# A grouped convolution ahead of a Strassen-like matrix product: the outer blocks of the convolution as one wider product in another bank, added by VectorE

## What is computed

```python
conv = lax.conv_general_dilated(x, weight, (1,), padding=[(4, 4)],      # x (32,128,2048), weight (128,32,9)
                                feature_group_count=4)                  # 4 groups of 32 channels, 9 taps
y = conv + einsum('nd,od->no', cond, c_weight)[:, :, None] + conv_bias[None, :, None]
base = matmul(y, kernel) + ffn_bias                                     # kernel (2048, 2048)
delta = B_eff @ (A_eff @ y) + lora_B_shared @ (lora_A_shared @ y)       # low rank parts, rank 32, per batch of 4 samples
out = x + base + delta
```

## Time and profile before

| | us |
|---|---|
| median of 3 runs | 1742.2 (1741.74 to 1744.91) |
| the profiled execution | 1747.0, span 1745.2 |
| TensorE busy | 1722.7 (99%) in 8666 matmuls |
| VectorE busy | 987.1 (57%) in 1260 instructions |
| ScalarE busy | 669.9 (38%) |
| mean granted clock of TensorE | 0.996 |

### The profile page before, as it was taken

One profiled execution on the slowest core, in us unless ns is written; L12 is line 12 of the kernel. 1 busy time (PEld: TensorE's weight loads), 2 busy tenths in 40 slices (PEclk: granted clock), 3 DMA queues, 4 the chain that ended last, 5 costly groups with the idle time before them and its releaser, 6 DMA issues.

```text
span 1745.2 us, 21990 instructions
## 1 busy us (share of the span) xinstructions
PE 1722.7 (99%) x8666; PEld 1460.6 (84%) x8666; DVE 987.1 (57%) x1260; ACT 669.9 (38%) x846; POOL 36.1 (2%) x70
## 2 busy tenths in 40 slices
PE   9999999999999999999999999999999999999998
PEld 6778888887888889999999888888888888888887
DVE  7647766664444578777665544355455554464443
ACT  6656666654222376555561221132233211121110
POOL 0001200000000000000000000000000000000000
PEclk9999999999999999999999999999999999999999
DMA  7859876656665656766665676568667798887764
GB/s 229 249 152 334 291 260 234 230 201 196 225 226 198 226 204 258 271 254 241 247 244 200 213 247 222 188 200 269 217 224 228 274 333 303 305 322 259 241 240 158
DMA packets 180143, 419.48 MB, mean 240 GB/s; under 512 B 50692, under 2 KB 90212, under 8 KB 175400
## 3 DMA queue, kind: packets, MB, share of 16 engines
q1 hardware_dynamic: 169960, 381.22, 64.1%
q0 software_dynamic: 9216, 33.56, 5.2%
q10 hardware_dynamic: 864, 3.29, 0.5%
HBM read 271.97 MB, written 146.03 MB: 240 GB/s over the span
## 4 chain that ended last, share of the span: by engine, by line
PE 89%; DMA 5%; DVE 3%; ACT 1%; issue 1%; SPq 0%; POOL 0%; ACTq 0%; DVEq 0%
PE acc L1430 65%; PE cps L1306 15%; PE acc L1337 3%; PE cps L1353 3%; DMA g<-in_L_ffn_kernel 2%; DMA T<-g 1%; DMA g<-in_L_ffn_lora_A 1%; ACT x_q L688 1%; PE acc L1385 1%; PE cps L1370 1%; DMA mixed_A<-g 1%; DVE x_q L946 0%; DMA st<-in_L_ffn_kernel 0%; DMA b_raw<-shared_B 0%; PE cps L1363 0%
## 5 line engine op out<-in xcount | busy, mean ns | idle before, releaser
L1430 PE MATMUL acc<-w_hi,y_t 128*128 128x512 f32 x3584 | 996.0, 392 | 1.8 <-DVE w_lo L938 1.8
L1430 PEld LDWEIGHTS acc<-w_hi,y_t 128*128 128x128 f32 x3584 | 666.5, 188 | 138.4 <-issue 2.7
L1430 PE MATMUL acc<-w_lo,y_t 128*128 128x512 f32 x1792 | 553.8, 390 | 0.0
L1430 PEld LDWEIGHTS acc<-w_lo,y_t 128*128 128x128 f32 x1792 | 337.2, 188 | 71.5
L688 ACT COPY x_q<-x_raw 32x512 f32<-32x512 f32 x248 | 268.4, 1082 | 16.2 <-DVE x_lo L952 13.4
L1306 PE MATMUL cps<-cw_hi,x_hi 128*128 128x384 f32 (+2 forms) x768 | 229.7, 299 | 3.3 <-DVE ax L1085 2.6
L1063 DVE TENSOR_TENSOR g<-acc,g 128x1024 f32<-128x1024 f32 x96 | 117.2, 1222 | 203.8 <-PE acc L1337 116.7
L1306 PE MATMUL cps<-cw_lo,x_hi 128*128 128x384 f32 (+2 forms) x768 | 229.8, 299 | 0.0
L1306 PE MATMUL cps<-cw_hi,x_lo 128*128 128x384 f32 (+2 forms) x768 | 229.2, 298 | 0.0
L727 ACT CAST y_t<-g 128x1024 fp32r<-128x1024 f32 x95 | 100.1, 1054 | 334.8 <-PE acc L1430 305.4
L1023 DVE TENSOR_TENSOR y_t<-g,y_t 128x1024 fp32r<-128x1024 f32 x95 | 116.0, 1221 | 109.8 <-ACT y_t L727 109.6
(11 more groups left out here) (117 smaller groups left out, 940.7 us busy)
## 6 DMA issues: line engine op xcount, KB each, us to landing
g<-A SPq DMA_DIRECT2D x80, 512.0 KB, 4.7
g<-U SPq DMA_DIRECT2D x80, 512.0 KB, 6.2
A<-g SPq DMA_DIRECT2D x64, 512.0 KB, 4.8
g<-in_x SPq DMA_DIRECT2D x64, 512.0 KB, 6.3
out<-g SPq DMA_DIRECT2D x64, 512.0 KB, 3.5
x_raw<-in_x SPq DMA_DIRECT2D x31, 1024.0 KB, 5.2
U<-g SPq DMA_DIRECT2D x48, 512.0 KB, 3.9
g<-in_L_ffn_kernel POOLq DMA_DIRECT2D x32, 512.0 KB, 8.6
```

What stands on the lines that cost most here:

```text
L1430: ins = T.matmul(acc[:, b, m, :], y_buf[b][:, c, part, :], wt[:, k % SLOTS, m * 512:(m + 1) * 512], start=(c == 0 and part == 0 and wt is ...
```

## The change

In 28 of the 32 convolutions (all but v = 0, 1, 16 and 17) the products of x_hi with both parts of the weights are taken out of the two outer blocks. `cw_hi` and `cw_lo` become the two halves of one buffer, so that a moving operand of 2x128 columns takes both parts; `apart(v, i)` does one such matmul for each outer block, into `acc[:, v % 2, i % 2]`, the bank pair that is not in use by product(v - 1). The remaining 14 matmuls of a group go into `cps` as before (of the outer blocks, x_lo with cw_hi).

The order on TensorE: groups 0 and 1, `apart` 0, group 2, `apart` 1, group 3, `apart` 2, `apart` 3. `apart` i now raises `conv_done`. There are two banks for four groups, so `apart` 2 and 3 wait until `y_evac` says that groups 0 and 1 were taken.

On VectorE each `y_group` gets two more operations: after L962 it adds the columns of the high part of the weights and then those of the low part, 128x256 each, to the two ends of the group's `y_conv`. Each waits for the one ahead of it, by `y_added`; the last raises `y_evac`.

```diff
+OUTER = (5, 0)
...
-        cw_hi = sb("cw_hi", [P, GR, 3, P], F32R)
-        cw_lo = sb("cw_lo", [P, GR, 3, P], F32R)
+        cw = sb("cw", [P, 2, GR, 3, P], F32R)
...
+        cw_hi, cw_lo = cw[:, 0], cw[:, 1]
+        cw_both = cw[:].rearrange("p a g d m -> p a g (d m)")
...
+        def outer_apart(v):
+            return v not in (0, 1, NP, NP + 1)
+        def added_index(v):
+            return v - 2 if v < NP else v - 4
...
                                 ctx_bias[:, v % 2, gr * GC:(gr + 1) * GC].unsqueeze(1).to_broadcast([P, WIN, GC]),
-                                ALU.add).then_inc(y_evac, 1)
+                                ALU.add).then_inc(y_added if outer_apart(v) else y_evac, 1)
+                if outer_apart(v):
+                    ends = y_conv.rearrange("p (a t) o -> p a t o", t=4)[:, 0:4:3, :, gr * GC:(gr + 1) * GC]
+                    apart = acc[:, v % 2, i % 2, :].rearrange("p (a h t o) -> p a h t o", a=2, h=2, o=GC)
+                    for part in range(2):
+                        dve.wait_ge(y_added, (2 * GR) * added_index(v) + 2 * i + part + 1)
+                        V.tensor_tensor(ends, apart[:, :, part], ends, ALU.add).then_inc((y_added, y_evac)[part], 1)
...
+            def apart(v, i):
+                gr = GROUPS[i]
+                if i >= 2:
+                    pe.wait_ge(y_evac, 4 * v + i - 1)
+                elif v < NP:
+                    pe.wait_ge(evac_act, v - 1)
+                else:
+                    pe.wait_ge(evac_dve, v - 1)
+                for blk, row, col, k0, k1, t0 in TAPS_OF:
+                    if blk in OUTER:
+                        n = 0 if t0 == 0 else 256
+                        ins = T.matmul(acc[:, v % 2, i % 2, n:n + 256], x_hi[:, gr, row, col:col + P],
+                                       cw_both[:, :, gr, k0 * GC:k1 * GC], start=True, stop=True)
+                ins.then_inc(conv_done, 1)
...
+                    if outer_apart(v) and i >= 2:
+                        apart(v, i - 2)
+                    n, last = 0, 13 if outer_apart(v) else 17
+                    for blk, row, col, k0, k1, t0 in TAPS_OF:
                         for xs, ws in ((x_hi, 0), (x_hi, 1), (x_lo, 0)):
+                            if outer_apart(v) and blk in OUTER and xs is x_hi:
+                                continue
                             ins = T.matmul(cps[:, gr, t0 * GC:(t0 + k1 - k0) * GC], xs[:, gr, row, col:col + P],
-                                           cw_strip[ws][:, gr, k0 * GC:k1 * GC], start=(n == 0), stop=(n == 17))
+                                           cw_strip[ws][:, gr, k0 * GC:k1 * GC], start=(n == 0), stop=(n == last))
                             n += 1
+                    if outer_apart(v):
+                        continue
...
+                if outer_apart(v):
+                    apart(v, 2)
+                    apart(v, 3)
```

More of the change, by code:

```diff
@@ L131, in build @@
         axd_words = axd_hl[:].bitcast(F32)
-        cw_strip = [w[:].rearrange("p g d m -> p g (d m)") for w in (cw_hi, cw_lo)]
+        cw_hi, cw_lo = cw[:, 0], cw[:, 1]
+        cw_strip = [w.rearrange("p g d m -> p g (d m)") for w in (cw_hi, cw_lo)]
+        cw_both = cw[:].rearrange("p a g d m -> p a g (d m)")
         wraw = b_raw[:, 0:GC * TAPS].rearrange("p (i k) -> p k i", k=TAPS)
@@ L239, in build @@
         y_evac = sem("y_evac")
+        y_added = sem("y_added")
         yc_out = [sem("yc_out0"), sem("yc_out1")]
@@ L1302, in conv @@
                         pe.wait_ge(ax_ready, NP + v - 1)
-                    n = 0
-                    for _, row, col, k0, k1, t0 in TAPS_OF:
+                    if outer_apart(v) and i >= 2:
+                        apart(v, i - 2)
+                    n, last = 0, 13 if outer_apart(v) else 17
+                    for blk, row, col, k0, k1, t0 in TAPS_OF:
                         for xs, ws in ((x_hi, 0), (x_hi, 1), (x_lo, 0)):
+                            if outer_apart(v) and blk in OUTER and xs is x_hi:
+                                continue
                             ins = T.matmul(cps[:, gr, t0 * GC:(t0 + k1 - k0) * GC], xs[:, gr, row, col:col + P],
-                                           cw_strip[ws][:, gr, k0 * GC:k1 * GC], start=(n == 0), stop=(n == 17))
+                                           cw_strip[ws][:, gr, k0 * GC:k1 * GC], start=(n == 0), stop=(n == last))
                             n += 1
+                    if outer_apart(v):
+                        continue
                     ins.then_inc(conv_done, 1)
```

## The result

The changed kernel takes 1791.1 us (median of 4, 1787.3 to 1791.8) against 1742.0 (median of 4, 1741.0 to 1744.9): ratio 1.0279, 95% interval 1.0265 to 1.0293, 2.8% slower. 1785 was forecast, with a range of 1766 to 1805. The profiled execution took 1791.4 with a span of 1789.6, against 1747.0 and 1745.2 before. The profiled execution of the kernel before lies 5 us above its kernel's median, so the spans differ by 44.4 and the medians by 49.1.

What follows compares the result with a forecast made beforehand. TensorE, busy 99% of the span, was taken to bound the kernel. Waits net of the saving, 29.7 us, plus 13.6 of clock loss gave 43, added to 1742.2: 1785 us, range 1766 to 1805.

Steps and rivals of the forecast that it cites:

- The saving: TensorE's outer blocks: one 256-column matmul replaces two of 128, saving 0.90 us per convolution, 25 us over 28.
- VectorE's price: Two dependent adds per group: 1.53 us from group to group, convolution ends 3.52 us after the emptying starts.
- Y stays: Y, from the start of L1135 (T) to VectorE's emptying, stays; only the forms' DMA waits, 16.5 us, get hidden.
- The sum of the waits: TensorE waiting for freed banks in the third and fourth wider products, saving included: +29.7 us over all convolutions.
- the old 4.7: v = 4 to 8 of the kernel before: 4.7 us of other waits, behind late emptyings or late forms, that go.
- The clock: TensorE's granted clock falls after idle gaps ahead of the third wider product: 13.6 us lost.
- the six long gaps: TensorE idling 2.5 to 5.4 us in v = 4 to 7, 10 and 13: 4x2.6+2x1.6 = 13.6 us of clock loss.
- the five short ones: TensorE idling 1.3 to 1.8 us in v = 8, 9, 11, 12, 14: taken as nothing, left open up to 8 us.
- The periods: Sign in the profile after, L1135 to L1135: 27 to 29 us in v = 4 to 7, 25 to 27 in v = 9 to 14.
- waits, but the clock stays up: Rival: TensorE waits for the banks but its granted clock does not fall; +30, 1772 us; chance 0.25.
- The clock falls in the short gaps too: Rival: short gaps also lower TensorE's clock, or the adds take longer than 0.424 us; 1803 us; chance 0.15.
- The wait never binds: Rival: emptying starts before T+5.3, T being L1135's start, and the saving is paid in full; -25, 1717 us; chance 0.03.

Runs made afterwards that it cites:

- e8: Changed kernel with VectorE's eight sample copies set between the groups' emptyings and the forms moved ahead of copy_mixed_B: 1721.7 us, ratio to the kernel before 0.9855.
- e10: Changed kernel with one VectorE add for each group in place of two, TensorE's work the same: 1763.4 us, ratio to the kernel before 1.0109.
- e3: Changed kernel with 151 useless matmuls filling TensorE's idle time ahead of the third wider product in v = 4 to 14: 1772.4 us, ratio to before 1.0158.
- e11: Changed kernel with useless matmuls filling the short gaps only, in v = 9, 11, 12 and 14: 1786.8 us, ratio to the kernel before 1.0246.
- e4: Changed kernel with VectorE's eight copies of the next sample set between the groups' emptyings: 1735.0 us, ratio to the kernel before 0.9940.
- e7: Kernel before, all 18 matmuls and no wider product, plus only VectorE's two adds and their waits in the 28 convolutions: 1748.9 us, ratio 1.0023.
- e9: Changed kernel with only the forms moved ahead of copy_mixed_B on VectorE, nothing interleaved: 1745.1 us, ratio to the kernel before 1.0005.

## Why the prediction was right, step by step

- **The saving.** 0.90 us a convolution was forecast, 25 in all; without waits it is 0.81 in phase 2 (9.69 to 8.88 in e8) and 0.80 in phase 0, 22.5 in all. The two wider products of a group take 0.29 us from their first start to the next other matmul in e8 (702.09 to 702.38), not 2x0.118. That alone would take 0.21 off the 0.90; what gives back 0.12 is not shown. The 81 ns of the Trainium skill ("TensorE: Matmul & The Clock Gate", Back-to-back issue gap) would have given 10 us, an estimate from the page. This case's traces do not agree with it: the row of before, 0.115 us for 128 columns, was the better guide.
- **VectorE's price.** 1.53 from group to group and 3.52 from the start of the emptying to product were both met to 0.01 us where the clock was up. They came out of two errors of opposite sign: release to matmul took 0.06 (362.68 to 362.74), forecast 0.15, and the two matmuls after a wait took 0.34, forecast 0.24. e10 shows the adds' part: two fewer in the chain, 0.9 us less.
- **Y stays.** In the changed kernel L1154 still waits 5.43 us in every period from v = 4 on, and L974 follows it by 7.9 to 9.5 us in v = 8 to 14, the same as before in v = 9 to 14 (v = 8 started at T+13.8 before). The DMA wait of the forms, 16.5 us, is 0 in v = 5 to 8, as forecast.
- **The sum of the waits.** v = 4 to 8: forecast 16.0, the convolutions grew by 21.2 and the old 4.7 went, 16.5. v = 9 to 14: forecast 13.8, measured 14.8 (in v = 9, 10, 11 and 13 the last two wider products took 0.54 to 0.60 us up to product's start, not 0.34, since the clock fell within them). v = 18 to 30: forecast 2.5, measured 1.8. The idle times themselves were 0.3 to 0.5 us shorter than forecast (1.0 to 1.5 in the short cases, not 1.3 to 1.8), since the main matmuls ended at T+8.5 and not at T+8.3, and TensorE started 0.1 us sooner after the release.
- **The clock: the term that was mis-sized.** 13.6 was forecast for the six long gaps (with 2.6 for each of four, where its row gave 2.7) and nothing for the five short ones; measured from what lies between the convolutions (13.54 before), the long ones lost 11.1 (1.1 to 2.6 each) and four of the short ones 5.8, 16.8 together. The prediction left the short gaps open and then put them at nothing; that is the step that failed. The 0.24 us of work between two gaps did not protect in ten of eleven periods. e3 shows the whole term by taking it away, 19.0 us with what was lost within the convolutions, e11 the part of the short gaps. The price itself was less certain than one row suggests: the gap of 2.65 us at convolution 16, from which the 1.6 was read, stands in every run and cost nothing in the changed kernel, e4, e7 and e9, 1.5 to 1.6 in the kernel before and six others, and 2.8 to 3.0 in e8 and e10. First matmul of convolution 16 and of product in the changed kernel, then in e8:

```profile
666.61 0.59 PE L1345 MATMUL cps<-cw,x_hi 128*128 128x384 f32 x2 [2.65 <-DVE ax L1104]
...
676.39 0.68 PE L1474 MATMUL acc<-w_hi,y_t 128*128 128x512 f32 x2
...
611.43 0.98 PE L1362 MATMUL cps<-cw,x_hi 128*128 128x384 f32 x2 [2.64 <-DVE ax L1120]
...
624.16 0.67 PE L1491 MATMUL acc<-w_hi,y_t 128*128 128x512 f32 x2
```

- **The periods.** 27 to 29 us were forecast in v = 4 to 7 and 25 to 27 in v = 9 to 14, and 29.7 to 31.3 and 26.6 to 28.1 measured: the list of signs left out the clock loss, of the long gaps too.
- **The end.** The eleven periods lost 48.1 us where 43.4 was forecast. What is not changed differs by some 4 us the other way, so the spans differ by 44.4, near the forecast of 43 partly by luck. The medians differ by 49.1, 6 more than forecast.

The rivals: "waits, but the clock stays up" was to give 1772, and e3, which is just that, measured 1772.4, but the changed kernel isn't there. "The clock falls in the short gaps too" was right in its first half. "The wait never binds" was to give 1717 with the emptying ahead of T+5.3; e8 makes that order and measures 1721.7.

Open: which of two equal gaps lowers the clock. v = 8, 12 and 14 had the same idle times in the changed kernel, and only v = 8 kept its clock; in e11 it lost it. Why e7 is 5.6 us slower by the medians when its eleven periods account for 1.2 also stays open; the profiled execution was 6 us faster than its kernel's median and does not show it. What all kernels share varies too: over the thirteen profiled executions convolution 3 starts between 99.2 and 104.6 us, and convolution 16 varies by 3 us.

## What to carry to other kernels

When a change gives work to an engine that is "only 57% busy" and makes the bound engine wait for it, its share says nothing: read when that engine starts this very work inside the period, and work out from there when each gate opens. What counts is what stands ahead of it in its list; moving a few instructions that TensorE does not wait for into an idle stretch of VectorE turned 1791 us into 1745, and with the copies spread as well into 1722. An idle gap of TensorE is dearer than its length: of the 48 us, 17 were clock lost after the gaps, though the same gap did not cost the same in every execution.

## What was not expected of the hardware

Two gaps of 1.0 us with one pair of wider products between them lowered TensorE's granted clock in some periods and not in others (a later product of 15.1 instead of 13.5 us), while a single gap of 1.0 us in e3 never did in eleven periods, nor one of 0.7 us in each of thirteen periods of phase 2. Useless matmuls in the first gap (6 for a gap of 1.0 us, 28 for 4.9) kept the clock at 1.00 and cost nothing. The two matmuls of 256 columns after a wait took 0.34 us up to the next start, those of e8 that waited for nothing 0.29, against 0.118 each in a row of such matmuls.
